# A decoder kernel's prologue: the first decay chain and the second norm handed between GpSimd and VectorE

## What is computed

```python
x = x + _L0_attn_ref(_layernorm(x, axis=-1), L0_attn_W_write, L0_attn_W_read, L0_attn_W_alpha, ...)
# inside, with rk the normed keys (two heads of 128), wk the keys moved by one row
beta = sigmoid(x @ W_beta.T)
log_decay = -exp(A_log) * softplus(x @ W_alpha.T + dt_bias)
cum = cumsum(log_decay, -1)                    # within chunks of 64
L_mask = tril(exp(tril(cum[:, None] - cum[None, :])))
M = tril(-(wk * beta) @ wk.T * L_mask, -1)
A = solve_triangular(eye - M, eye)
```

## Time and profile before

| | us |
|---|---|
| median of three runs | 5426.35 |
| lowest, highest | 5419.66, 5430.18 |
| the profiled execution | 5424.35 |
| its span, first to last instruction | 5421.6 |
| VectorE, GpSimd, TensorE busy in the span | 4177.1, 4005.8, 4688.4 |
| loop, from about 319 us on | 5102 |

### The profile page before, as it was taken

One profiled execution on the slowest core, in us unless ns is written; L12 is line 12 of the kernel. 1 busy time (PEld: TensorE's weight loads), 2 busy tenths in 40 slices (PEclk: granted clock), 3 DMA queues, 4 the chain that ended last, 5 costly groups with the idle time before them and its releaser, 6 DMA issues.

```text
span 5421.6 us, 105836 instructions
## 1 busy us (share of the span) xinstructions
PE 4688.4 (86%) x28201; PEld 3073.6 (57%) x28362; DVE 4177.1 (77%) x10963; ACT 2323.3 (43%) x4480; POOL 4005.8 (74%) x11220
## 2 busy tenths in 40 slices
PE   1059998999999899999989999898999999899998
PEld 1045664656566565656656565565656556565655
DVE  7068787787887778788787878778787887778788
ACT  0034444444444444444444444444444444444344
POOL 7878676786867678686767868677786867768686
PEclk7589999999999999999999999999999999999999
DMA  3000000000000000000000000000000000000000
GB/s 97 0 13 1 29 1 13 17 9 21 1 25 5 9 21 9 21 1 25 5 9 21 7 23 1 25 5 9 21 1 29 1 25 5 9 21 1 21 1 17
DMA packets 61879, 78.07 MB, mean 14 GB/s; under 512 B 11168, under 2 KB 53808, under 8 KB 61232
## 3 DMA queue, kind: packets, MB, share of 16 engines
q1 hardware_dynamic: 52784, 62.42, 3.5%
q10 hardware_dynamic: 8448, 8.39, 0.4%
HBM read 45.04 MB, written 8.46 MB: 10 GB/s over the span
## 4 chain that ended last, share of the span: by engine, by line
POOL 36%; PE 28%; DVE 17%; issue 11%; ACT 4%; POOLq 3%; DMA 0%; DVEq 0%; ACTq 0%; SPq 0%
POOL acc_c L584 12%; POOL arena L584 7%; POOL acc_a L584 3%; POOL acc_b L584 3%; PE bank L1280 3%; POOL acc_s L584 3%; POOL sl_t L584 3%; POOLq L583 3%; PE bank L1016 2%; DVE arena L2018 2%; PE bank L1187 2%; PE bank L1023 2%; PE bank L1140 2%; PE bank L1106 2%; ACT arena L779 2%
## 5 line engine op out<-in xcount | busy, mean ns | idle before, releaser
L1784 DVE TENSOR_REDUCE smax<-bank 128x4 f32<-128x512 f32 x768 | 524.4, 683 | 92.1 <-PE bank L1098 31.8
L766 ACT ACTIVATE arena<-bank 128x512 f32<-128x512 f32 x768 | 454.8, 592 | 248.4 <-PE bank L1106 242.6
L1788 DVE TENSOR_TENSOR arena<-bank,smax 128x512 f32<-128x512 f32 x768 | 530.8, 691 | 26.4
L1106 PE MATMUL bank<-ident,arena 128*128 128x128 f32 x3072 | 484.8, 280 | 45.1 <-ACT arena L753 28.1
L1092 PE MATMUL bank<-arena 64*128 64x512 f32 x1536 | 439.2, 648 | 64.4 <-ACT arena L790 28.0
L1187 PE MATMUL bank<-w,arena 128*128 128x512 f32 x1024 | 480.0, 599 | 14.0 <-DVE arena L1736 14.0
L1106 PEld LDWEIGHTS bank<-ident,arena 128*128 128x128 f32 x3072 | 345.7, 141 | 245.0 <-ACT arena L755 82.3
L1220 PE MATMUL bank<-w,arena 128*128 128x256 f32 x2048 | 454.1, 380 | 13.9 <-ACT arena L825 13.9
L753 ACT ACTIVATE arena<-arena,rstd 128x512 f32<-128x512 f32 x512 | 368.2, 719 | 201.4 <-DVE arena L1788 196.8
L1220 PEld LDWEIGHTS bank<-w,arena 128*128 128x128 f32 x2048 | 387.8, 190 | 90.3 <-issue 23.0
L584 POOL TENSOR_TENSOR acc_a<-acc_s,arena 128x32 f32<-128x32 f32 x1008 | 264.6, 262 | 171.6 <-DVE row L1347 47.2
(11 more groups left out here) (428 smaller groups left out, 11813.6 us busy)
## 6 DMA issues: line engine op xcount, KB each, us to landing
arena<-in_x_dram SPq DMA_DIRECT2D x35, 512.0 KB, 3.6
xn_next<-arena SPq DMA_DIRECT2D x17, 512.0 KB, 2.9
arena<-cum_dram SPq DMA_DIRECT2D x17, 512.0 KB, 3.6
arena<-in_ctx_dram SPq DMA_DIRECT2D x16, 512.0 KB, 3.7
out_dram<-arena ACTq DMA_DIRECT2D x16, 512.0 KB, 3.1
xn<-xn_next SPq DMA_DIRECT2D x15, 512.0 KB, 3.1
w<-in_L_ffn_w_dram SPq DMA_DIRECT2D x8, 512.0 KB
w<-in_L_ffn_w_dram SPq DMA_DIRECT2D x1, 1024.0 KB
```

What stands on the lines that cost most here:

```text
L766: act.activation(PT[:, v % 2], bank[3 + v % 2][:, :].rearrange("p (h q) -> p h q", h=QH), ACT.Copy).then_inc(S["pt"], 1)
L1106: ins = tr(bank[3 + v % 2][:, j * P:(j + 1) * P], Ssb[:, v % 4, j, :], ident[:, :])
L1784: dve.tensor_reduce(smax[:, u, :], sc, AX, ALU.max).then_inc(S["s_max"], 1)
L1788: dve.tensor_tensor(Ssb[:, u % 4], sc, smax[:, u, :].unsqueeze(2).broadcast_to([P, QH, P]), ALU.subtract).then_inc(S["s_sub"], 1)
```

## The change

Only instructions in front of the loop are changed.

- GpSimd makes the products of all four slices one after the other into four pairs of buffers (`slice_pe`), 88 instructions, and no longer the links.
- VectorE runs the links: for each slice it waits for that slice's products (`first_step`), and then makes the 16 groups. Between them it does `key_limit` (second slice), `beta_rows` (third) and the second norm's root (fourth, behind four groups). It ends the chain and makes `au`.
- GpSimd, behind the products, makes the second norm's sums (`second_sums`), waits for VectorE's root (`ref_step`, now 134 steps) and makes the quotient (`second_quotient`), 18 instructions on 128x1024. Then come the sums of batch 2 and the decay table, as before.
- VectorE's `first_norm(1)` is gone. `key_rows` stands behind `decay_column`; on TensorE `key_features` and `gram` stand behind `decay_columns`; on ScalarE the second `variance_seed` stands behind `key_scale`, and `row_copies` and `beta_exp` in front of it.

```diff
+        slice_pe = [[unit(u, lo, DH * G * SLICE).rearrange("p (h b d) -> p h b d", b=G, d=SLICE) for lo in (0, DH * G * SLICE)] for u in (24, 7, 9, 0)]
+        quo1, high1, low1, prod1, rest1, term1 = (cut(u, G, D) for u in (16, 22, 3, 5, 6, 8))
...
             for j in range(SLICES):
-                chain_products(pool, first_link, xn0[:, :, :], j)
-                chain_links(pool, first_link, j, 0, 16)
-            chain_end(pool, first_link)
-            pool.wait_ge(first_step, first[0])
-            pool.tensor_tensor(au[:, :], acc_a[:, :, 0], acc_a[:, :, 1], ALU.add).then_inc(au_ready, 1)
+                chain_products(pool, first_link, xn0[:, :, :], j, pe=slice_pe[j])
...
+            def second_sums():
+
+                tt = pool.tensor_tensor
+                pool.wait_ge(loaded_x, 32)
+                first_link(tt, lan[:, :, :], x_in[:, :, 0:16], x_in[:, :, 16:32], ALU.add)
+                for k in range(2, D // 16):
+                    first_link(tt, lan[:, :, :], lan[:, :, :], x_in[:, :, 16 * k:16 * k + 16], ALU.add)
...
+                first_link(tt, x_in[:, :, :], x_in[:, :, :], row[:, 0, :].unsqueeze(2).broadcast_to([P, G, D]), ALU.subtract)
+                w8 = sq.rearrange("p b (k n) -> p b k n", n=32)
+                first_link(tt, sq, x_in[:, :, :], x_in[:, :, :], ALU.mult)
+                first_link(tt, lan2[:, :, :], w8[:, :, :, 0], w8[:, :, :, 1], ALU.add)
+                for k in range(2, 32):
+                    first_link(tt, lan2[:, :, :], lan2[:, :, :], w8[:, :, :, k], ALU.add)
...
+            def second_quotient():
+
+                tt, xs = pool.tensor_tensor, x_in[:, :, :]
+                over = lambda n: row[:, n, :].unsqueeze(2).broadcast_to([P, G, D])
+                pool.wait_ge(ref_step, REF_BEFORE)
+                first_link(tt, quo1, xs, over(5), ALU.mult)
+                first_link(tt, term1, quo1, splitter[:, :].unsqueeze(2).broadcast_to([P, G, D]), ALU.mult)
+                first_link(tt, high1, term1, quo1, ALU.subtract)
+                first_link(tt, high1, term1, high1, ALU.subtract)
+                first_link(tt, low1, quo1, high1, ALU.subtract)
+                first_link(tt, prod1, quo1, over(4), ALU.mult, known=True)
+                first_link(tt, rest1, high1, over(7), ALU.mult, known=True)
+                first_link(tt, rest1, rest1, prod1, ALU.subtract)
+                for q, n in ((high1, 8), (low1, 7), (low1, 8)):
+                    first_link(tt, term1, q, over(n), ALU.mult)
+                    first_link(tt, rest1, rest1, term1, ALU.add)
+                first_link(tt, xs, xs, prod1, ALU.subtract)
+                first_link(tt, xs, xs, rest1, ALU.subtract)
+                first_link(tt, term1, xs, over(5), ALU.mult)
+                pool.wait_ge(first_step, first[0])
+                tt(xs, term1, quo1, ALU.add).then_inc(x_norm, 1)
+
+            second_sums()
+            second_quotient()
             centered(0, 0)
...
-            variance_seed(1)
             key_squares(0, 0, moved_now, xn0)
-            key_scale(0, 0)
             row_copies(0, 0)
+            beta_exp(0, 0)
+            key_scale(0, 0)
+            variance_seed(1)
             key_copies(0, 0)
-            beta_exp(0, 0)
...
-            key_features(0, 0)
             beta_columns(0, 0)
-            gram(0, 0)
             decay_rows(0, 3)
             decay_columns(0, 3)
+            key_features(0, 0)
+            gram(0, 0)
...
-            first_norm(1)
-            assert run["ref"] == REF_BEFORE, run["ref"]
-            dve.wait_ge(moved_now, 16)
-            key_limit(0, 0)
-            key_rows(0, 0, xn0)
-            beta_rows(0, 0)
...
+            for j in range(SLICES):
+                dve.wait_ge(first_step, PRODUCTS * (j + 1))
+                chain_links(dve, first_link, j, 0, 4, slice_pe[j])
+                if j == 1:
+                    key_limit(0, 0)
+                if j == 2:
+                    beta_rows(0, 0)
+                if j == 3:
+                    run["n"] = 1
+                    exact_root_seed()
+                    exact_root()
+                    assert run["ref"] == REF_BEFORE, run["ref"]
+                chain_links(dve, first_link, j, 4, 16, slice_pe[j])
+            chain_end(dve, first_link)
+            dve.wait_ge(set_dve, n_set[0])
+            dve.tensor_tensor(au[:, :], acc_a[:, :, 0], acc_a[:, :, 1], ALU.add).then_inc(au_ready, 1)
...
             decay_column(3)
+            dve.wait_ge(moved_now, 16)
+            key_rows(0, 0, xn0)
             first_level(0, 0)
...
-REF_BEFORE = 224
+REF_BEFORE = 134
```

More of the change, by code:

```diff
@@ L389, in _, with chain_products @@
             exchange_decays(NIT + 1)
-        def chain_products(eng, link, src, j, first=0, last=PRODUCTS):
-            tt, count = eng.tensor_tensor, [0]
+        def chain_products(eng, link, src, j, first=0, last=PRODUCTS, pe=(sp_p, sp_e)):
+            tt, count, (prod, rest) = eng.tensor_tensor, [0], pe
             def product(*operands, known=False):
@@ L408, in chain_products, with chain_links @@
                 w, wh, wl = (d[:, h, j * SLICE:(j + 1) * SLICE].unsqueeze(1).broadcast_to([P, G, SLICE]) for d in (dw[0], dw[1], dw[2]))
-                product(sp_p[:, h], xs, w, ALU.mult)
-                product(sp_e[:, h], sl_h, wh, ALU.mult, known=True)
-                product(sp_e[:, h], sp_e[:, h], sp_p[:, h], ALU.subtract)
+                product(prod[:, h], xs, w, ALU.mult)
+                product(rest[:, h], sl_h, wh, ALU.mult, known=True)
+                product(rest[:, h], rest[:, h], prod[:, h], ALU.subtract)
                 for a1, b1 in ((sl_h, wl), (sl_l, wh), (sl_l, wl)):
                     product(sl_t[:, :, :], a1, b1, ALU.mult, known=b1 is wl and a1 is sl_h)
-                    product(sp_e[:, h], sp_e[:, h], sl_t[:, :, :], ALU.add)
+                    product(rest[:, h], rest[:, h], sl_t[:, :, :], ALU.add)
             assert count[0] == PRODUCTS, count[0]
-        def chain_links(eng, link, j, first, last):
+        def chain_links(eng, link, j, first, last, pe=(sp_p, sp_e)):
             tt, flat = eng.tensor_tensor, "p h b d -> p (h b) d"
-            pf, ef = sp_p.rearrange(flat), sp_e.rearrange(flat)
+            pf, ef = pe[0].rearrange(flat), pe[1].rearrange(flat)
             for k in range(first, last):
@@ L566, in _ @@
             for j in range(SLICES):
[L567 to L571 removed]
+                chain_products(pool, first_link, xn0[:, :, :], j, pe=slice_pe[j])
+                assert first[0] == PRODUCTS * (j + 1), first[0]
@@ new lines, in second_sums @@
+            def second_sums():
[4 more added lines that the diff above has]
+                    first_link(tt, lan[:, :, :], lan[:, :, :], x_in[:, :, 16 * k:16 * k + 16], ALU.add)
+                l4 = lan[:, :, :].rearrange("p b (c d) -> p b c d", d=4)
+                m4 = lan2[:, :, :].rearrange("p b (c d) -> p b c d", d=4)
+                first_link(tt, m4, l4[:, :, 0:4:2, :], l4[:, :, 1:4:2, :], ALU.add)
+                first_link(tt, lan[:, :, 0:4], lan2[:, :, 0:4], lan2[:, :, 4:8], ALU.add)
+                first_link(tt, lan2[:, :, 0:2], lan[:, :, 0:4:2], lan[:, :, 1:4:2], ALU.add)
+                first_link(tt, row[:, 0, :], lan2[:, :, 0], lan2[:, :, 1], ALU.add)
+                first_link(tt, row[:, 0, :], row[:, 0, :], one_row[:, 0:1].broadcast_to([P, G]), ALU.mult)
+                first_link(tt, x_in[:, :, :], x_in[:, :, :], row[:, 0, :].unsqueeze(2).broadcast_to([P, G, D]), ALU.subtract)
[4 more added lines that the diff above has]
+                    first_link(tt, lan2[:, :, :], lan2[:, :, :], w8[:, :, :, k], ALU.add)
+                first_link(tt, lan[:, :, 0:4], lan2[:, :, 0:4], lan2[:, :, 4:8], ALU.add)
+                first_link(tt, lan2[:, :, 0:2], lan[:, :, 0:4:2], lan[:, :, 1:4:2], ALU.add)
+                first_link(tt, row[:, 1, :], lan2[:, :, 0], lan2[:, :, 1], ALU.add)
+                first_link(tt, row[:, 1, :], row[:, 1, :], one_row[:, 0:1].broadcast_to([P, G]), ALU.mult)
+                pool.wait_ge(first_step, first[0])
+                tt(row[:, 1, :], row[:, 1, :], eps_ln[:, 0:1].broadcast_to([P, G]), ALU.add).then_inc(ref_var, 1)
@@ L1643, in _, with first_link @@
             assert n_set[0] == SET_DVE, n_set[0]
-            first_norm(1)
-            assert run["ref"] == REF_BEFORE, run["ref"]
-            dve.wait_ge(moved_now, 16)
-            key_limit(0, 0)
-            key_rows(0, 0, xn0)
-            beta_rows(0, 0)
+            def first_link(operation, *operands, known=False, behind=0):
+                if not known:
+                    dve.wait_ge(set_dve, n_set[0] - behind)
+                operation(*operands).then_inc(set_dve, 1)
+                n_set[0] += 1
+            for j in range(SLICES):
[14 more added lines that the diff above has]
+            dve.tensor_tensor(au[:, :], acc_a[:, :, 0], acc_a[:, :, 1], ALU.add).then_inc(au_ready, 1)
             for part in range(10):
```

4 lines of the change are left out of this document (2 added, 2 removed).

## The result

The changed kernel takes 5414.25 us (median of nine runs, 5405.82 to 5419.4) against 5426.44 (nine runs, 5419.66 to 5431.64): ratio 0.9974, 95% interval 0.9964 to 0.9984. That is faster by 14 us by the ratio, where 36 were predicted and 5378 to 5408 was the range. The near end of the interval is a gain of 0.16%, less than the 0.2% that the prediction counted as no change: a gain is shown, but hardly more than a measurement can tell.

What follows compares the result with a forecast made beforehand. The prediction took GpSimd's first chain to bound the prologue. Ending it at 249.5 us gained 33.5, the decay formula another 3, together 36: span 5385.6, execution 5388, against the median 5390, range 5378 to 5408 us.

Steps and rivals of the forecast that it cites:

- What bounds, and what is worth something: Prologue: GpSimd's first chain ends it; at most the 160.7 us in which only GpSimd works could be gained.
- Links beside GpSimd: First chain: VectorE makes 105 links under GpSimd's products, bounds 88 to 123, and 88 under the second norm's sums.
- the middle: Links under GpSimd's products: 105, taken midway between 88 and 123.
- GpSimd isn't slowed: Products beside VectorE's links: GpSimd keeps its pace, so its products end at 122.3 us.
- Links with nothing beside them: VectorE alone after 145.8 us: 216 links at 0.20 us take 43.2, and the root ends at 194.7.
- The quotient: Second norm on GpSimd: 18 instructions of 128x1024 at 1.97 us, 35.5 us, ending at 230.2.
- the prediction's own list: Closing signs against it: au at 265 or more, quotient instructions over 2.2 us each, or a changed loop length.
- The decay formula: VectorE behind the chain: 19.2 us instead of 22.3, as two held additions are past; another 3 us gained.
- Steps moved: Key scaling behind the decay column: hidden by 13.6 us of cover, 2.5 to spare, cost 0; 10 us without cover.
- The step that failed: Loop behind the prologue: the same program in both kernels, so only the earlier end of the series is counted.
- the first paragraph: The prediction's opening on what bounds the kernel: the prologue, about 320 us of 5421.6, ends with GpSimd's first chain.
- The sum: Prologue times added up: chain ends at 249.5, 33.5 us gained, with the decay formula 36; nothing for TensorE's clock.

Runs made afterwards that it cites:

- a_vg2: The a_vg kernel a second time, in more rounds and with a second profile: ratio 0.992 to the kernel before, 5384.66 us against 5427.92.
- a_vg: Changed kernel plus 94 one-column memsets on VectorE and 45 on GpSimd, restoring both loops' places modulo 128: ratio 0.9944 to the kernel before, 5397.27 us.
- b_128: Kernel before plus 128 one-column memsets each on VectorE and GpSimd: ratio 0.9999 to the kernel before.
- a_128: Changed kernel plus 128 one-column memsets each on VectorE and GpSimd: ratio 0.9966 to the kernel before.
- b_vg: Kernel before plus 34 one-column memsets on VectorE and 83 on GpSimd, its loops at the changed kernel's places modulo 128: ratio 1.006, 5453.98 us against 5424.59.

## Why the prediction was right and wrong

- **What bounds, and what is worth something**: right. The end of the first chain set the start of the loop; it moved and the loop's start moved with it.
- **Links beside GpSimd**: right. Forecast were 105 links (88 to 123) by the end of the products; 119 were made, since more of them slipped in than the middle, and 98 for 88 under the second norm's sums. The rows at 78.76 show the pattern: one link of 0.19 starts with the product and ends freely, the next is held to its end. "GpSimd isn't slowed" was off: with two links under it a product takes 0.78 and not 0.72, and the products end at 124.2, not 122.3.
- **Links with nothing beside them**: right. 193 links, the beta rows and the root took from 149.2 to 192.0, the root's 22 instructions 4.4 us of it, 2.7 us ahead of the forecast 194.7. Links come in steps of 0.22, and pairs in steps of 0.12 and 0.10:

```profile
186.70 0.18 DVE L1700 TENSOR_TENSOR acc_d<-arena,acc_b 128x32 f32<-128x32 f32 x1
186.82 0.19 DVE L1700 TENSOR_TENSOR acc_c<-acc_s,acc_c 128x32 f32<-128x32 f32 x1
187.04 0.19 DVE L1700 TENSOR_TENSOR acc_c<-acc_c,acc_d 128x32 f32<-128x32 f32 x1
187.27 0.19 DVE L1700 TENSOR_TENSOR acc_c<-acc_c,arena 128x32 f32<-128x32 f32 x1
```

  The Trainium skill's statement weighed there ("VectorE: DVE Perf Modes", The DRAIN you can't avoid), that leaving out semaphores between instructions saves nothing, doesn't hold for these small additions: 0.12 from start to start without a wait against 0.22 with one.
- **The quotient**: mis-sized. 18 x 1.97 = 35.5 forecast, 40.3 measured (192.0 to 232.3). The price was the step between two instructions of which one subtracts a broadcast row (1.91) and the other multiplies a tile by itself (1.89); ten of the eighteen have two different full tiles and cost a quarter more:

```profile
L563 POOL TENSOR_TENSOR arena<-arena 128x1024 f32<-128x1024 f32 x9 | 21.3, 2370 | 0.7
L563 POOL TENSOR_TENSOR arena<-arena,row 128x1024 f32<-128x1024 f32 x7 | 13.4, 1926 | 43.1 <-DVE row L1398 42.8
```

  It costs nothing, as VectorE makes 33 links meanwhile and the links set the end. By the prediction's own list ("over 2.2 us each") that is a sign against it, and the end came out right all the same: the root was 2.7 us early, and the first use of `au` came 3.9 us ahead of the forecast 249.5.
- **The decay formula**: 19.2 us forecast, 22.1 measured (245.59 to the end of the sums at 267.74). The two additions held by 128x1024 instructions, which I had taken as past by then, are held still, for 1.74 us each, because the chain ended earlier than forecast and GpSimd's two instructions later (the load landed at 238.6 for 236.7). Errors of 3.9 and 2.9 us nearly cancel, and the exchange took 5.1 for 4.75: table at 272.9, forecast 273.5. That the table is off by only 0.6 us is luck; the terms ahead of it are off by up to 5.
- **Steps moved**: right. Scaling the keys begins at 268.85, the first level waits for the decay table (11.59 us, released by GpSimd) and not for the Gram matrix.
- **The step that failed** stands in the first paragraph: "The loop behind is the same program in both kernels and starts when this series ends, so I count only how much earlier the series ends." The program is the same, its time is not. The sum had no term for it, and no rival either; it stood only in the last list, as what would prove me wrong. The prologue ends 37.3 us earlier and 14 are left, so it is worth 23 us here, and by the table 24, two thirds of the gain. TensorE's clock, on which the sum put nothing, played no part in the prologue, but the loss came with that clock in the loop: 279 us at 1.2 GHz instead of 218.
- With the loop back at its place modulo 128 the gain is about the forecast one: a_vg2 gives 0.992, 43 us, and a_vg, the same program, 0.9944, 30 us, a mean of 37 for 36 forecast. Repeats that lie 13 us apart can't confirm a sum to 1 us; that the sum was sound and its scope too small rests on the start of the loop, 37.3 us earlier for 36.

## What to carry over

A change ahead of a long loop moves the loop's code. In this kernel, where TensorE's granted clock falls at a few places of each turn, that alone took back or gave some 25 us of 5400, nearly as much as the change is about. Before believing a small gain or loss of such a change, run both kernels with a few dozen idle instructions more, and with 128 more as a control, and compare the loops' own lengths in the profiles as well as the totals. In a forecast, give the loop behind a change a term of its own with both signs. Here the changed prologue with 94 and 45 empty instructions (a_vg2) is the fastest of all, 0.992 of the kernel before.

## What the runs showed of the hardware

- **Every 128th instruction comes late.** On GpSimd 0.06 to 0.12 us (numbers 67 modulo 128 in the traces' count), on VectorE 0.11 to 0.13 at the mark above, and 0.41 when instructions come every 0.03 us. This is a_vg2's row of 94 empty instructions, which breaks behind the 61st, VectorE's 63rd instruction:

```profile
0.88 1.75 DVE L1649 MEMSET pad_v<- 128x1 f32 x61 [0.88 <-PEq L2133]
3.04 0.97 DVE L1649 MEMSET pad_v<- 128x1 f32 x33 [0.41 <-issue]
```

  The part on queues in the changed kernel's page of the profile has two that carry instructions, with 3.46 MB in 422 packets and 3.93 MB in 240, 8.2 and 16.4 KB each:

```profile
q8 instruction: 240, 3.93, 0.3%
q14 instruction: 422, 3.46, 0.2%
```

  The start times of q14's packets in the traces tie them to the late instruction. In the kernel before GpSimd passes a number 67 modulo 128 in the loop 144 times, and each time a packet of 8.2 KB starts within 1.5 us; behind instructions far from such a number one does so in 6% of cases. Over all twenty profiles it is 2905 of 3024. For VectorE's number 63 it is 124 of 144 in the kernel before and 67 of 144 in the changed one, against 7 to 8%. The packet starts behind the late instruction (in the kernel before 0.74 us behind number 67, in the median), so the instruction isn't waiting for this packet: it marks the passage from one block of code to the next. How the passage makes the instruction late is open.

  The Trainium skill gives 64 bytes as an instruction's width ("Vector Engine (DVE) Microarchitecture Reference", 1.2 Instruction fetch and dispatch); by that, as an estimate, 8.2 KB are 128 of them, and q8's 16.4 KB are 256. The Trainium skill's page "Runtime: NRT & Kernel Launch", Instruction fetch mechanics, speaks of blocks of 256 and says that the fetch is hidden. For GpSimd and VectorE the runs differ on both: 128 instructions more left both marks in place (b_128, a_128), and the passage costs 0.06 us or more.
- **Idle filler isn't free on GpSimd.** In b_vg a run of 83 one-column memsets held a 128x4 instruction of VectorE from its start to the run's end, 2.61 us instead of 0.17, and the loop began 2.8 us later:

```profile
29.26 2.80 POOL L566 MEMSET pad_g<- 128x1 f32 x83
...
29.48 2.61 DVE L1349 TENSOR_SCALAR row<-row 128x4 int32<-128x4 int32 x1
```
